# Attended values of a wide attention: one matmul over both sequences of a tile, or one for each half of the array's rows

## The reference, cut to what matters

```python
def _cross_attention(q_in, kv_in, wq, bq, wk, bk, wv, bv, wo, bo, bias_k, bias_v):
    ...
    qh = (q_in @ wq + bq).reshape(b, q_len, H, K)
    kh = (kv_in @ wk + bk).reshape(b, t, H, K)
    vh = (kv_in @ wv + bv).reshape(b, t, H, K)
    kh = jnp.concatenate([kh, jnp.broadcast_to(bias_k, (b, 1, H, K))], axis=1)
    vh = jnp.concatenate([vh, jnp.broadcast_to(bias_v, (b, 1, H, K))], axis=1)
    ...
    logits = jnp.einsum('bqhk,bthk->bhqt', qh, kh) / scale
    weights = jax.nn.softmax(logits, axis=-1)
    ctx = jnp.einsum('bhqt,bthk->bqhk', weights, vh).reshape(b, q_len, H * K)
    return ctx @ wo + bo
```

## Time and profile before

| | |
|---|---|
| median of 3 runs | 2432.32 us (2425.67 to 2437.57) |
| the profiled execution's own time | 2433.81 us |
| its span, first to last instruction | 2432.0 us |
| PE busy | 2240.4 us (92%), 15,874 instructions |
| PEld busy | 1774.0 us (73%) |
| DVE busy | 1236.7 us (51%) |
| ACT busy | 959.8 us (39%) |
| POOL busy | 320.7 us (13%) |

### The profile page before, as it was taken

How to read it: one execution, slowest core, us unless ns; L and a number is a source line. 1 busy time by engine, 2 the same in 40 slices (tenths; PEclk the granted TensorE clock), 3 DMA queues, 4 the chain that set the end, 5 groups by cost and what they waited for, 6 DMA issues and landing times. The chain is left out here.

```text
span 2432.0 us, 41151 instructions
## 1 busy us (share of the span) xinstructions
PE 2240.4 (92%) x15874; PEld 1774.0 (73%) x15874; DVE 1236.7 (51%) x2696; ACT 959.8 (39%) x2593; POOL 320.7 (13%) x626
## 2 busy tenths in 40 slices
PE   6899898999998999999999799999999979788975
PEld 5778787787776777777777577777777767666753
DVE  6857775765561333333333233333333326888686
ACT  2343345545343333333333233333333334444442
POOL 1011111000000000000000000000000013333340
PEclk9999999999999999999999899999999989898987
DMA  6000000020004200000000300000000010000000
GB/s 233 4 15 28 15 21 14 21 96 13 7 10 159 76 13 13 13 13 0 13 13 5 74 5 13 13 13 13 0 13 13 5 31 1 10 9 6 9 1 14
DMA packets 60088, 62.98 MB, mean 26 GB/s; under 512 B 16000, under 2 KB 57024, under 8 KB 58304
## 3 DMA queue, kind: packets, MB, share of 16 engines
q1 hardware_dynamic: 59968, 61.29, 7.8%
HBM read 50.79 MB, written 10.49 MB: 25 GB/s over the span
## 5 line engine op out<-in xcount | busy, mean ns | idle before, releaser
L1415 ACT ACTIVATE l2a_exps<-l2a_ps_s,l2a_shift 128x65 f32<-128x65 f32 x512 | 154.5, 315 | 299.8 <-DVE l2a_shift L1475 299.8
L1404 ACT ACTIVATE l2a_qT<-l2a_ps_q,cols 128x256 f32<-128x256 f32 x256 | 107.6, 471 | 392.9 <-PE l2a_ps_q L1549 392.9
L1601 PE MATMUL l2a_ps_y<-shared,l2a_oT 128*128 128x256 f32 x1024 | 242.4, 380 | 1.1 <-ACT l2a_oT L1421 1.1
L1463 DVE TENSOR_SCALAR l2a_kT<-l2a_ps_k,cols 128x256 f32<-128x256 f32 x256 | 112.1, 480 | 194.6 <-PE l2a_ps_k L1549 193.5
L1601 PEld LDWEIGHTS l2a_ps_y<-shared,l2a_oT 128*128 128x128 f32 x1024 | 184.6, 190 | 21.3 <-ACT l2a_oT L1421 1.5
L1489 DVE COPY l2a_pT<-l2a_ps_p 64x256 f32<-64x256 f32 x256 | 107.9, 421 | 122.4 <-PE l2a_ps_p L1580 120.7
L1471 DVE TENSOR_REDUCE l2a_row_max<-l2a_ps_s 128x4 f32<-128x260 f32 x128 | 54.9, 429 | 191.7 <-PE l2a_ps_s L1572 191.7
L1590 PE MATMUL l2a_ps_o<-l2a_pT,l2a_v 128*128 128x128 f32 x1024 | 148.1, 288 | 0.0
L1378 POOL TENSOR_TENSOR l2a_learned<-l2a_exps,l2a_inv_sum 128x4 f32<-128x4 f32 x128 | 26.1, 204 | 872.2 <-DVE l2a_probs L1482 872.2
L1590 PEld LDWEIGHTS l2a_ps_o<-l2a_pT,l2a_v 128*128 128x128 f32 x1024 | 124.0, 191 | 8.8
L1549 PEld LDWEIGHTS l2a_ps_k<-l2a_cT,l_wk 128*128 128x128 f32 x512 | 97.9, 191 | 38.3 <-issue 27.8
(11 more groups left out here) (265 smaller groups left out, 4413.8 us busy)
## 6 DMA issues: line engine op xcount, KB each, us to landing
f_c_tile<-in_ctx SPq DMA_DIRECT2D x16, 256.0 KB, 2.8
between<-f_final SPq DMA_DIRECT2D x16, 256.0 KB, 2.2
l2a_c_tile<-in_ctx SPq DMA_DIRECT2D x16, 256.0 KB, 2.7
shared<-in_l_wo SPq DMA_DIRECT2D x2, 2048.0 KB, 17.7
inside<-l2a_y_out SPq DMA_DIRECT2D x16, 256.0 KB, 2.2
f_x_tile<-in_x SPq DMA_DIRECT2D x8, 256.0 KB, 7.2
shared<-in_l_w SPq DMA_DIRECT2D x2, 1024.0 KB, 9.4
l_mlp_w<-in_l_mlp_w SPq DMA_DIRECT2D x2, 1024.0 KB, 10.2
```

Source lines behind the costliest of these rows:

```text
L1404: last = nc.scalar.activation(qT[:, n, :], ps_q[:, n * ROUND:(n + 1) * ROUND], ACT.Identity, bias=col(f"l2_bq{a + 1}", 2 * p + n), scale=1.0)
L1415: nc.scalar.activation(exps[:, m, :], ps_s[:, m * KEYS:(m + 1) * KEYS], ACT.Exp, bias=shift[:, m:m + 1], scale=scale, accum_out=row_sum[:, ...
L1463: last = nc.vector.tensor_scalar(kT[:, n, :, 0:SEQ], ps_k[:, n * ROUND:(n + 1) * ROUND].rearrange("d (m k) -> d m k", k=SEQ), col(f"l2_bk{ ...
L1601: nc.tensor.matmul(ps_y[:, u * DIM:(u + 1) * DIM], oT[:, n, u].rearrange("d b q -> d (b q)"), wo[:, 2 * p + n, :], start=(p == 0 and n == ...
```

## The change

The attended values are computed for each sequence by itself. `pT` loses its third axis and with it the zeros and their memset, so `set_up` counts one less. In `attend` each of the 4 matmuls becomes two: for u = 0 on rows 0 to 63 of the array and for u = 1 on rows 64 to 127, each with 64 keys of `v` (all 128 features) in the array and 64 columns of `pT` streaming. The two write to two banks (`o_half`): u = 0 to columns 0 to 255 of bank o, u = 1 to columns 256 to 511 of bank p. `attended_out` makes one copy for each bank. Since bank p is now written by `attend` and read by ACT, `transpose_probs` waits for the `o_ready` of the pair before, and the learned transposes move from bank p to bank x.

```diff
--- before.py
+++ after.py
@@ -1258,13 +1258,14 @@
         inv_sum = sb("inv_sum", [P, 2 * NU])
         learned = sb("learned", [P, NU, P])
         learnedT = sb("learnedT", [P, NU, P])
-        pT = sb("pT", [P, 2 * NB, NU, SEQ])
+        pT = sb("pT", [P, 2 * NB, SEQ])
         oT = sb("oT", [P, 2, NU, NB, SEQ])
         res_b = sb("res_b", [P, 2, DIM])
         y_out = sb("y_out", [P, 2, DIM])
         value_gap = sb("value_gap", [P, HEADS, ONES + 1])
         gap_out = sb("gap_out", [P, DIM])
         ps_q, ps_k, ps_v, ps_s, ps_p, ps_o, ps_y, ps_x = (bank(n) for n in "qkvspoyx")
+        o_half = [ps_o[:, 0:ROUND], ps_p[:, ROUND:2 * ROUND]]
         norm = Normed(nc, sb, sem, x_tile, ps_x, lambda c: col(f"l2_ln{a}_s", c), lambda c: col(f"l2_ln{a}_b", c), ident)
         hT = norm.hT
 
@@ -1359,10 +1360,9 @@
             nc.gpsimd.memset(value_gap[:], 0.0).then_inc(set_up, 1)
             nc.gpsimd.memset(gap_out[:], 0.0).then_inc(set_up, 1)
             nc.gpsimd.memset(learned[:], 0.0).then_inc(set_up, 1)
-            nc.gpsimd.memset(pT[:], 0.0).then_inc(set_up, 1)
+            pool.wait_ge(set_up, 5)
+            nc.gpsimd.memset(learned[:, :, ONES:ONES + 1], 1.0).then_inc(set_up, 1)
             pool.wait_ge(set_up, 6)
-            nc.gpsimd.memset(learned[:, :, ONES:ONES + 1], 1.0).then_inc(set_up, 1)
-            pool.wait_ge(set_up, 7)
             norm.inverse_deviations(pool, 0)
 
             def learned_key(i, p):
@@ -1417,14 +1417,14 @@
 
             def attended_out(i, p):
                 act.wait_ge(o_in_psum, per_pair(i, p))
-                for n in range(2):
-                    last = nc.scalar.activation(oT[:, n], ps_o[:, n * ROUND:(n + 1) * ROUND].rearrange("d (b u q) -> d u b q", b=NB, u=NU),
+                for u in range(NU):
+                    last = nc.scalar.activation(oT[:, :, u].rearrange("d n b q -> d n (b q)"), o_half[u].rearrange("d (n t) -> d n t", n=2),
                                                 ACT.Copy)
                 last.then_inc(o_ready, 1)
 
             def learned_transposed(i):
                 act.wait_ge(learnedT_in_psum, count(i, 1, 0))
-                nc.scalar.activation(learnedT[:].rearrange("h u q -> h (u q)"), ps_p[:, ROUND:2 * ROUND], ACT.Copy
+                nc.scalar.activation(learnedT[:].rearrange("h u q -> h (u q)"), ps_x[:, 0:ROUND], ACT.Copy
                                      ).then_inc(learnedT_ready, 1)
 
             def slot(i, j, made, attended, projected, more):
@@ -1486,7 +1486,7 @@
                 dve.wait_ge(pT_in_psum, per_pair(i, p))
                 for u in range(NU):
                     half = slice(u * SEQ, (u + 1) * SEQ)
-                    last = nc.vector.tensor_copy(pT[half, :, u, :], ps_p[half, 0:ROUND].rearrange("k (m q) -> k m q", q=SEQ))
+                    last = nc.vector.tensor_copy(pT[half], ps_p[half, 0:ROUND].rearrange("k (m q) -> k m q", q=SEQ))
                 last.then_inc(pT_ready, 1)
 
             def add_residual(i):
@@ -1515,7 +1515,7 @@
                 if j == 3 and more:
                     norm.normalised(dve, i + 1)
                 if j == -1:
-                    dve.wait_ge(set_up, 7)
+                    dve.wait_ge(set_up, 6)
                     dve.wait_ge(folded_in_psum, 1)
                     nc.vector.tensor_copy(gap_out[0:ONES + 1, :], ps_y[0:ONES + 1, 0:DIM]).then_inc(folded_ready, 1)
                     dve.wait_ge(folded_ready, 1)
@@ -1576,6 +1576,10 @@
 
             def transpose_probs(i, p):
                 pe.wait_ge(p_ready, per_pair(i, p))
+                if p:
+                    pe.wait_ge(o_ready, per_pair(i, p - 1))
+                elif not isinstance(i, int) or i:
+                    pe.wait_ge(o_ready, per_pair(i - 1, PAIR - 1))
                 for n in range(2):
                     last = nc.tensor.transpose(ps_p[:, n * P:(n + 1) * P], probs[:, n * NU:(n + 1) * NU, :].rearrange("q u k -> q (u k)"), ident)
                 last.then_inc(pT_in_psum, 1)
@@ -1587,9 +1591,12 @@
                     pe.wait_ge(v_ready, value_event(i, g, 1))
                 for n in range(2):
                     for b in range(NB):
-                        last = nc.tensor.matmul(ps_o[:, n * ROUND + b * P:n * ROUND + (b + 1) * P],
-                                                v[g % 2][b][:, (first + n) * WIDE:(first + n + 1) * WIDE],
-                                                pT[:, n * NB + b].rearrange("k u q -> k (u q)"), start=True, stop=True)
+                        at = n * NB + b
+                        for u in range(NU):
+                            keys_of = slice(u * SEQ, (u + 1) * SEQ)
+                            last = nc.tensor.matmul(o_half[u][:, at * SEQ:(at + 1) * SEQ],
+                                                    v[g % 2][b][keys_of, (first + n) * WIDE:(first + n + 1) * WIDE],
+                                                    pT[keys_of, at], start=True, stop=True)
                 last.then_inc(o_in_psum, 1)
 
             def project_out(i, p):
@@ -1604,7 +1611,7 @@
             def learned_value(i):
                 pe.wait_ge(learned_ready, per_pair(i, PAIR - 1))
                 for u in range(2):
-                    last = nc.tensor.transpose(ps_p[:, ROUND + u * P:ROUND + (u + 1) * P], learned[:, u, :], ident)
+                    last = nc.tensor.transpose(ps_x[:, u * P:(u + 1) * P], learned[:, u, :], ident)
                 last.then_inc(learnedT_in_psum, 1)
 
             def add_learned_value(i):
```

## The result

The changed kernel took 2445.45 us (median of 7 runs, 2443.09 to 2447.67), the kernel before 2428.67 (7 runs, 2424.56 to 2437.57): a ratio of 1.0066, 95% interval 1.005 to 1.0082, so 16.8 us slower. Run once more beside its own reference on another chip it came to 1.0057 (1.0036 to 1.0079). The forecast was 2452, the range 2438 to 2468, and slower by over 0.5% the likeliest.

A forecast was written before the change was run, and what follows sets the result against it. PE, busy 92% of the span, was taken to bound the kernel by the sum of its passes. 148 ns more per attend block, x 128 = +18.9 us, gave 2451.2 us against the runs' median, stated as 2452, range 2438 to 2468.

The forecast's parts named there:

- What bounds the kernel: In the two `wide_attention` calls PE is busy without gaps, so the sum of its passes sets the end.
- Pace set by the load: Attend passes take at least their load's columns plus some 4 ns, 111 ns for 128 columns, though the stream is halved.
- Row groups run side by side: Loads and streams of the attend's two 64-row groups run together, offset about 6 ns.
- halves in turn: Rival: attend's two row halves are served one after the other, +0.89 us a block, 2566 us in all; chance 0.06.
- the bound of a late second half: Attend's second half served late behind the scores: at most 54 ns a block, +6.9 us; taken as 0.
- The attend block, 1,036 ns: From the attend's first load to the next block's load: 16 passes, last stream and drain take 1,036 ns.
- The drain of 92 ns: At the attend's exit to the full array, 92 ns pass before the next load, as behind the scores.
- The exposed load, 107 ns: Behind each attend block the next block's first load is not hidden and costs 107 ns.
- The sum, +18.9 us: Exit costs less the shorter last stream give 148 ns an attend block, x 128 = +18.9 us.
- The last attend of a call: It pays a drain at entry, 0.2 us with its load, its exit lies in PE's waiting; together zero.
- Wait, bank x, copies, memset: The `o_ready` wait, moved learned transposes, changed ACT and DVE copies and dropped `pT` memset each change the time by zero.
- Code and clock: Grown PE code stays resident and the clock holds, costing zero; the rival that either costs time had chance 0.02.

The follow-up runs named there:

- experiment 1: Kernel before, each attend pass streaming only the first sequence's 64 columns, ACT copying its values in place of the second's: 0.9992 of the kernel before.
- experiment 3: Changed kernel with each attend matmul cut into two 64-value column halves, 32 passes on four array quarters, waits ahead of scores: 2399.16 us, 0.9867 of the kernel before.
- experiment 4: Changed kernel with all eight attend passes of the first row half issued ahead of all eight of the second: 2511.37 us, 1.0327 of the kernel before.
- Experiment 9: Changed kernel with the transposes of the learned weights moved from behind the attend to ahead of the scores: 2445.04 us in one run.
- Experiment 5: Kernel before plus the change's wait for `o_ready` ahead of the transposes and its learned transposes in bank x, attend unchanged: 0.9992 of the kernel before.

## Why the prediction was right, point by point

- **What bounds the kernel: right.** PE's idle time in the stretches didn't change, and the time moved by what the blocks on PE moved.
- **Pace set by the load, "however short the stream": right, and the core of it.** Pairs 0.11 us apart in the changed kernel; experiment 1 shows it without any other change, and experiment 3 from the other side. The Trainium skill (TensorEngine Tiling, Overview) gives up to 2x where the contracted dimension is 64 or less; the row halves with their loads of 128 columns gained nothing of that: the block went from 0.99 us to 1.04, the kernel to 1.0066. Cutting the loaded columns as well took the block from 0.99 us to 0.63, or 0.73 with the exit that it adds. The sentence of the same skill that a load's time goes by its columns (TensorE: Matmul & The Clock Gate, the section on LDWEIGHTS) agrees among the loads of weights: 188 ns for 64 rows, 192 for 128, and 135 for the 64 columns of the quarters. The loads ahead of transposes, 140 ns for 128 columns, stand apart from it.
- **Row groups run side by side: right,** offset under 10 ns, forecast 6. The "halves in turn" rival and the bound of a late second half came to nothing in this order of issue; experiment 4 shows that they were not idle fears: with another order of the same passes the second half does start late.
- **The attend block, 1,036 ns forecast: 1.038 measured.** The drain of 92 ns, taken from the scores, is in it: of the 0.26 us from the last load to the next block's, 107 ns are the load and 54 the last stream (both by the prediction's rate a column), which leaves 0.09 to 0.10.
- **The exposed load, 107 ns: 0.102 ahead of the values, and 0.055 ahead of transposes** (their block takes 0.273 us at the median and took 0.218). Here a term of the sum was mis-sized: at 16 of 128 exits, 14 of them in the stretches, it took a transpose's load at the price of a load of weights, so that the slot of 9.04 us became 9.14 and not 9.19. The trace of the kernel before could have told: its loads ahead of the learned transposes last 142 ns, not 192. Experiment 9 moved the transposes away, and these slots grew by the missing 0.046.
- **The sum, +18.9 us: 17.3 in the stretches.** A slot grew by 0.145 us instead of 0.148 at 110 exits (0.3 us less) and by 0.100 at the 14 with learned transposes (0.7 less). The last two exits of each call stand where PE waits; the sum counted them all the same (0.6 less). The last of the 63 distances changed by -0.005 us: that exit costs nothing.
- **The last attend of a call: not zero.** The prediction saw that it now pays a drain at its entry, and put entry and exit at nothing together. It starts 0.09 us later behind the transposes than before and ends 0.15 later, and PE then waits for ACT's copy of it: the projection comes 3.96 us behind the transposes instead of 3.81, some 0.15 us a call. That it comes to as much as an exit that the sum counted there is luck.
- **Wait, bank x, copies, memset: zero, right.** Experiment 5 for the wait and the bank. DVE and ACT are busy as long as before in the stretches (206.7 and 214.8 us for 206.9 and 215.4), and nothing on PE waits for `l2a_oT` ahead of the transposes. The memset's 0.5 us can't be told from the scatter ahead of the calls.
- **Code and clock: no cost, right.** Clock 1.00 in the stretches, and from 900 to 1300 us of the changed kernel again only queue 1 moves data, 4,080 packets. One slice of the earlier trace rows in the middle of the calls isn't at 9 but at 7, with the clock at 8: it holds the 8.3 us between the calls, and the changed kernel's page has the same.
- **The stated time was 2452, 6.5 us above.** Of that 1.6 is the sum's, 3.6 the base (2432.3 was the median of three runs, 2428.67 that of seven), 0.8 the rounding up from 2451.2, and the rest scatter. The bounds for the pace, -1.8 and +0.9 us, were too wide: the whole-array block goes at the same pace, so only one step of it is left in the difference, 0.3 us.

What stays open: drain and exposed load were seen apart in the timeline, but no run removed one and kept the other. The 0.09 and the 0.10 are therefore a split of one cost by its timeline. And the line of three passes is read from starts: it was made for one run and foretold a second, and no record shows it.

## What to carry to other kernels

Where the stream is shorter than the load, price a block of matmuls by its loads: columns loaded times the rate, however few rows they fill (188 and 192 ns here) and however few columns stream; a split that only shortens the stream or empties rows gains nothing, one that shortens the load does. Count each change of the array's shape as a cost of its own, here 0.09 us of drain and 0.05 to 0.10 for the load that is no longer hidden, and look for the neighbour that makes it cheap (0.100 us ahead of transposes, 0.145 ahead of the values). Where a block is split over parts of the array, issue to them in turn, and compare a stretch of the trace that the change touches rather than the spans: in the changed kernel it repeats to 0.01 us where the spans scatter by several. Look at its slots as well: in experiment 4 the two stretches differ by 1.65 us, all of it in one slot.

## What the runs showed of the hardware

- Passes on different row halves start out of the order of the program: in experiment 4 the second half's first pass (1008.34) starts ahead of the first half's sixth (1008.45), seventh and eighth. Eight passes in a row on one half hold up the other by 0.50 us, four in a row by 0.01 at the start of a block and 0.05 later. A line of three passes beyond the one under way would explain both; it is not shown.
- Four quarters of 64 by 64 run side by side, each some 7 ns behind the one before it, at 58 ns a pass on each: 32 passes of load and stream start in 0.48 us, one each 15 ns.
- A load ahead of a transpose lasts 0.14 us where one of the same 128 by 128 for a matmul lasts 0.19 (medians 140 and 188 to 192 ns), and leaves 0.055 us open behind a drain instead of 0.102.
